# A routed expert stage on one core: where its visit map is made, how its shared map is spread, and in which order its merged tiles are stored

## What is computed

```python
mod = (_silu(c) @ wmod)                      # sa, ca, ga, sb, cb, gb per batch
h = _layernorm(x) * (1 + ca) + sa
x = x + ga * attention(h)                    # 16 heads, softmax over 256 tokens
h = _layernorm(x) * (1 + cb) + sb
logits = h @ router_w
e = argmax(logits);  weight = softmax(logits)[e]
hid = gelu(h @ w1[e] + b1[e])                # 128 -> 256
x = x + gb * weight * (hid @ w2[e] + b2[e])  # 256 -> 128
```

## Time and profile before

| | us |
|---|---|
| median of three runs | 622.87 |
| the profiled execution, its own time | 624.31 |
| its span, first to last instruction | 622.5 |
| VectorE busy | 564.3 (91%) |
| ScalarE busy | 542.3 (87%) |
| GpSimd busy | 483.0 (78%) |
| TensorE matmul busy | 471.1 (76%) |
| mean granted TensorE clock, share of full speed | 0.645 |

### The profile page before, as it was taken

The page is one execution under the profiler, slowest core; times in us unless marked ns, Lnnn a source line. Parts: engine busy times, 40 slices in busy tenths (PEclk is TensorE's granted clock), DMA queues, the critical chain, the costliest instruction groups (busy, mean ns, idle before and its releaser), DMA issues.

```text
span 622.5 us, 11883 instructions
## 1 busy us (share of the span) xinstructions
PE 471.1 (76%) x2535; PEld 265.6 (43%) x2537; DVE 564.3 (91%) x1432; ACT 542.3 (87%) x2310; POOL 483.0 (78%) x642
## 2 busy tenths in 40 slices
PE   5457877877887787788787887788776876799990
PEld 2113333433333343343343443343332465688980
DVE  5899999999999999999999999999999787878983
ACT  2599999999999999999999999999999745467760
POOL 4476777998899899999988999898887754567544
PEclk9555567566556756655556556655655589999996
DMA  6465454555555545554555456665553128857741
GB/s 190 106 185 149 135 137 129 151 148 150 148 155 147 157 143 150 144 153 141 140 141 145 135 148 178 181 169 155 152 168 127 51 97 222 274 176 203 230 124 34
DMA packets 77071, 94.41 MB, mean 152 GB/s; under 512 B 12806, under 2 KB 60710, under 8 KB 76998
## 3 DMA queue, kind: packets, MB, share of 16 engines
q1 hardware_dynamic: 68842, 75.69, 45.0%
q0 software_dynamic: 6144, 16.82, 7.2%
q10 hardware_dynamic: 2015, 1.15, 0.7%
HBM read 58.41 MB, written 35.20 MB: 150 GB/s over the span
## 4 chain that ended last, share of the span: by engine, by line
ACT 47%; POOL 18%; DVE 14%; issue 8%; PE 6%; DMA 4%; SPq 1%; DVEq 1%; ACTq 1%; POOLq 0%
ACT scores L887 46%; POOL table L804 3%; DVE neg_max L1339 3%; POOL xhat L753 2%; POOL rstd L736 2%; DVE y_biased_s L1910 2%; POOL rest L545 1%; POOL parts L548 1%; PE scores L1167 1%; DMA x_s<-table 1%; POOL out_dram L862 1%; PE scores L1176 1%; POOL h_scaled L776 1%; DMA table<-rows,place_i 1%; SPq L556 1%
## 5 line engine op out<-in xcount | busy, mean ns | idle before, releaser
L887 ACT ACTIVATE scores<-scores,neg_max 128x256 f32<-128x256 f32 x1024 | 467.5, 838 | 11.1 <-DVE neg_max L1339 11.0
L887 ACT ACTIVATION_READ_ACCUMULATOR scores<-scores,neg_max 128x1 f32 x1024 | 432.2, 599 | 0.0
L1339 DVE TENSOR_REDUCE neg_max<-scores 128x4 f32<-128x1024 f32 x256 | 309.2, 1211 | 7.1 <-PE scores L1019 6.5
L1019 PE MATMUL scores<-k_stack,q_stack 64*128 64x256 bf16 x1024 | 148.3, 388 | 79.0 <-ACT scores L887 68.5
L1019 PEld LDWEIGHTS scores<-k_stack,q_stack 64*128 64x128 bf16 x1024 | 33.9, 106 | 163.7 <-ACT scores L887 118.9
L804 POOL DMA_INDIRECT table<-rows,place_i x64 | 66.1, 1032 | 20.5 <-issue 17.1
L862 POOL DMA_INDIRECT out_dram<-out_room,x_s x51 | 49.8, 976 | 37.3 <-DVE out_room L1923 29.3
L1176 PE MATMUL scores<-w_s,hid 128*128 x308 | 50.5, 287 | 5.1 <-DVE y_biased_s L1910 3.2
L753 POOL TENSOR_SCALAR xhat<-rows,mv,rstd 128x128 f32<-128x128 f32 x60 | 47.5, 794 | 7.1 <-POOL rstd L736 7.1
L1047 PE MATMUL side_a<-w_gated,opt_t 128*128 128x128 f32 x128 | 49.8, 491 | 0.0
L745 POOL TENSOR_SCALAR xhat<-x_s,mv,rstd 128x128 f32<-128x128 f32 x62 | 49.0, 798 | 0.4 <-POOL rstd L736 0.4
(11 more groups left out here) (224 smaller groups left out, 878.7 us busy)
## 6 DMA issues: line engine op xcount, KB each, us to landing
x_s<-table SPq DMA_DIRECT2D x77, 192.5 KB, 3.0
q_stack<-parts_dram SPq DMA_DIRECT2D x192, 64.0 KB, 2.9
parts_dram<-parts SPq DMA_DIRECT2D x31, 384.0 KB
k_stack<-parts_dram SPq DMA_DIRECT2D x186, 64.0 KB, 2.3
mod_b<-mod_rows SPq DMA_DIRECT2D x32, 256.0 KB, 4.4
x_s<-in_x_dram SPq DMA_DIRECT2D x13, 256.0 KB, 5.0
table<-pad_tile SPq DMA_DIRECT2D x15, 192.5 KB
w1x_s<-in_w1x_dram SPq DMA_DIRECT2D x7, 258.0 KB, 4.6
```

The source lines that it names most:

```text
L887: last = act.activation(buf[:, k * L:k * L + L], buf[:, k * L:k * L + L], ACT.Exp, bias=neg_max[:, p, n:n + 1], accum_out=exp_sum[:, p, n: ...
L1019: last = pe.matmul(scores[:, c, at:at + L], q_stack[p][r, g + j, t * P:t * P + P], k_stack[p][r, g + j, :], start=True, stop=True)
L1339: dve.tensor_reduce(to, scores[:, (PAIRS * b.n + i) % RING, :].rearrange("p (e j m) -> p e j m", e=2, j=2), AX_X, ALU.max, negate=True).th ...
```

## The change

Three edits, and nothing of the arithmetic is altered.

1. **The map.** `map_counts()`, `map_rows()` and `map_columns()` leave tiles 6 to 8 and are run in `drain()`, behind `weigh_rows(last)` and the w1 fetch of visit 4, so ahead of DVE's share in visit 2. PE turns the map at the head of tile 7, DVE writes it out in tile 6.
2. **The shared map.** The same fourteen steps run one per tile in tiles 12 to 25. PE turns the result at the end of tile 28, DVE writes it out in tile 30.
3. **The stores.** Merged tile k waits for `min(k + 14, 2k + 2)` merges and stands in POOL's order directly behind the visit that brings that count; six merged tiles then stand between whole ones (visits 36 to 63), seven behind them (visits 64 to 76). Merged stores count on a semaphore of their own, for which SP waits last.

```diff
-MAP_TURNED = 9
-SHARED_AT = 15
-SHARED_TURNED = SHARED_AT + 9
+MAP_TURNED = 7
+SHARED_AT = 12
+SHARED_TURNED = SHARED_AT + 16
...
-def merged_by(slot):
+def merged_by(k):
-    return slot - WHOLE + E
+    return min(k + E, 2 * k + 2)
+def stores():
+    order, packed = [], 0
+    for q in range(NT):
+        f, v = VISITS[q]
+        if f is not None:
+            order.append((f, None))
+        while packed < PACKED and v is not None and merged_by(packed) == v + 1:
+            order.append((None, packed))
+            packed += 1
+    return order
...
-                sp.wait_ge(out_stored[s], 16 * len(range(s, T, SLOTS)))
+                sp.wait_ge(out_stored[s], 16 * len(range(s, WHOLE, SLOTS)))
+            sp.wait_ge(packed_stored, 16 * PACKED)
...
+            def store_packed(k):
+                pool.wait_ge(merged, merged_by(k))
+                pool.indirect_dma_start(out_rows, bass.IndirectOffsetOnAxis(ap=packed[:, k, D:OUT], axis=0),
+                                        packed[:, k, 0:D].bitcast(F32), None).then_inc(packed_stored, 16)
...
-            for n in range(FIRST, T):
-                store(n)
+            for n, k in STORES[FIRST:]:
+                if n is not None:
+                    store(n)
+                else:
+                    store_packed(k)
...
             def tile(j, s, turn):              # PE
+                if j == MAP_TURNED:
+                    turn_map()
                 if j == EARLY:
                     pe.wait_ge(map_ready, 1)
...
-                if j == MAP_TURNED:
-                    turn_map()
-                if j == SHARED_TURNED:
-                    turn_shared()
...
                     contract(j - AT_W2)
+                if j == SHARED_TURNED:
+                    turn_shared()
...
-                if j == MAP_TURNED:            # DVE
+                if j == MAP_TURNED - 1:
                     take_map()
...
-                    if n == FIRST:
-                        map_counts()
...
-                if j == SHARED_AT:
-                    shared_rest()
-                    shared_rest_f()
...
-                if n == PRIMED - 1:
-                    map_rows()
-                if n == PRIMED:
-                    map_columns()
+                steps_shared = (shared_rest, shared_rest_f, shared_places, shared_places_i, shared_split, shared_split_f, shared_spans,
+                                shared_before, shared_bounds, shared_low, shared_high, shared_in, shared_columns, shared_edges)
+                if 0 <= j - SHARED_AT < len(steps_shared):
+                    steps_shared[j - SHARED_AT]()
...
                 weigh_rows(last)               # DVE, drain
                 load_experts(PRIMED, EARLY - PRIMED)
                 fetch_w1(PRIMED)
+                map_counts()
+                map_rows()
+                map_columns()
```

More of the change, by code:

```diff
@@ L244, in shared_reload @@
     return min(SLOTS, SHARED - v) if v is not None and v % SLOTS == 0 else 0
-def merged_by(slot):
-    return slot - WHOLE + E
+def merged_by(k):
[10 more added lines that the diff above has]
+    return order
+STORES = stores()
+assert len(STORES) == T
 def early_slots(b):
@@ L508, in build_adaln_attention_moe @@
         merged = sem("merged")
+        packed_stored = sem("packed_stored")
         rows_loaded = [sem(f"rows_loaded{s}") for s in range(SLOTS)]
@@ L853, in store @@
             def store(n):
[L855 to L858, removed]
-                else:
[L860 to L863, removed]
-            over_batches(iteration, drain)
-            for n in range(FIRST, T):
-                store(n)
+                q = AT_VISIT[n]
+                pool.wait_ge(out_ready, q + 1)
+                pool.indirect_dma_start(out_rows, bass.IndirectOffsetOnAxis(ap=rows_in[q % SLOTS][:, ID:ROW].bitcast(I32), axis=0),
+                                        out_s[q % SLOTS][:, :], None).then_inc(out_stored[n % SLOTS], 16)
+            def store_packed(k):
+                pool.wait_ge(merged, merged_by(k))
+                pool.indirect_dma_start(out_rows, bass.IndirectOffsetOnAxis(ap=packed[:, k, D:OUT], axis=0),
+                                        packed[:, k, 0:D].bitcast(F32), None).then_inc(packed_stored, 16)
+            over_batches(iteration, drain)
+            for n, k in STORES[FIRST:]:
+                if n is not None:
+                    store(n)
+                else:
+                    store_packed(k)
         @block.scalar
```

## The result

The changed kernel took 615.98 us (median of six runs, 615.35 to 619.01), the kernel before beside it 622.61 (620.76 to 623.65): a ratio of 0.9902, 95% interval 0.9879 to 0.9926. The forecast was 615.7. The profiled execution of the changed kernel has a span of 613.5 and a time of its own of 615.35, the lowest of its six; that of before (624.31) lies above its median. The two profiles are thus 9.0 apart where the medians are 6.6 apart, and the sum has to be read from places inside them.

The account below looks back on a forecast made before the run. No engine is full in the visits; late rows bound visit 12, POOL's stores visit 48, POOL alone the end. Terms 0, -5.0, +0.5, -2.7 sum to -7.2: 624.31 becomes 617.1, median 615.7, range 612.0 to 620.3.

Parts of the forecast that it names:

- 0 for the map: Before visit 12: map about 2.9 us earlier, but the rows' scatter ends later, so no gain.
- -5.0: Shared map, visits 12 to 48: earlier single steps and later turn gain 5.0 us, bounds 3.5 to 6.7.
- +0.5: Six merged stores between whole ones push POOL's stores where it is backlogged: 0.5 us lost, bounds 0 and 2.5.
- -2.7: At the end, the last merged tile is stored right after the last merge: 2.7 us gained.
- the price of visits 7 to 11: TensorE before visit 12: five visits at 1.15 us each, 5.8, plus up to 0.9 waiting for a bias.
- the rival of the falling clock: TensorE stands longer before visit 12 and its clock falls, costing 2.1 us: 617.8 us; chance 8%.
- Visit 12 "well before 522": Sign of being wrong: visit 12 starting well before 522, where the forecast had its row wait ending near 522.8.
- POOL idled behind merged stores: Sign of being wrong: POOL idle behind merged stores while whole tiles are ready.
- load 38 waited for the shared map: Sign of being wrong: SP's load of visit 38 waiting for the shared map, despite a forecast cover of 1.6 us.
- The early scatter: Rival before visit 12: scatter lands before the map, visit 12 gains up to 2.9 more, 612.8 us; chance 8%.
- Only the end pays: Rival: w1 fetches or full DMA engines cancel the shared map's gain, leaving only the tail, 620.2 us; chance 13%.
- The slower rival: Merged stores waiting at the head of POOL's queue, 11.4 us in all, lose 9.0: 629.2 us; chance 5%.

Follow-up runs that it names:

- e2: Kernel before with the shared map's edit alone, old map place and old store order: 619.59 us, ratio 0.9949.
- e4: Changed kernel with all whole tiles stored first, then the merged ones at their new, lower merge counts: 615.87 us, ratio 0.9894.
- e3: Kernel before with the edit of the stores alone, map and shared map as before: 619.40 us, ratio 0.9946.
- e8: Changed kernel with the first six merged tiles stored later, five of them two whole tiles later and the last one: 617.54 us, ratio 0.9899.
- e10: Changed kernel with all whole tiles stored first and the shared map's steps begun in tile 8, turned in tile 24: 616.68 us, ratio 0.9880.
- e6: Changed kernel with the six pad blocks beside the last scatter moved, all fourteen written in visits 16 to 35: 620.42 us, ratio 0.9950.
- e9: Changed kernel with one more w1-sized copy on VectorE, into unused memory, in each of tiles 12 to 25: 619.23 us, ratio 0.9932.
- e1: Changed kernel with the map put back into tiles 6 to 8 and turned in tile 9: 617.10 us, ratio 0.9918.
- e5: Changed kernel with the shared map's steps back in tiles 15 to 22, up to two a tile, turn kept late: 619.44 us, ratio 0.9931.

## Why the prediction was right, and where not

**The sum.** The forecast was -7.2, of it 0 for the map, -5.0, +0.5, -2.7. Read from the places: -0.73 up to visit 12; store 32 -4.24 and visit 48 -4.11; from visit 48 to the end of the last merge +1.42 (40.88 to 42.30); from there to the last store -2.76 (3.13 to 0.37). That is -6.2, beside -6.6 between the medians. So the terms were off by -0.7, +0.9 (at visit 48), +0.9 and -0.1, 1.0 in all, and that 615.98 lies only 0.3 from the forecast median is in part luck. The stated bounds, 613.0 to 618.5, don't come out of the terms either: with 0 for the map their ends add up to -9.5 and -3.6, 613.4 to 619.3 on the median of 622.87.

**The map: the value was right, the reason half right.** The map did end earlier (written out at 511.85 instead of 517.55), and the stall fell from 3.18 to 0.70. The forecast said that the time comes back as a longer wait for visit 12's rows. That failed: the wait fell from 2.22 to 0.71. By the forecast's own figures TensorE was to be ready 8.3 us after the scatter's issue (520.9 - 512.55) and the rows 10.2 after it, 1.9 apart. Measured were 8.8 (518.55 - 509.77) and 9.5. So 0.7 of the missing cover is the quicker landing and what follows it, and 0.4 is TensorE. There the step at fault is the price of visits 7 to 11, 1.15 a visit. After the map's turn at 511.28 TensorE needed until 519.26 - 0.71 = 518.55, 7.3, where the forecast had 5.8 and up to 0.9 of waiting. In these stretches of after and of before:

```profile
510.00:514.00 4.00, 3.25 (x16) 2.53 (x16) 3.43 (x18) 1.29 (x5) 1.03 (x2) 0.50 1.03 296
```
```profile
510.00:514.00 4.00, 3.45 (x27) 3.05 (x27) 3.43 (x15) 2.40 (x10) 2.20 (x3) 1.00 0.55 187
```

the granted clock is 0.50, the lower level of 1.2 GHz, in after, and 1.00, 2.4 GHz, in before. So time went into slow visits in front of the wait, and the wait for the rows hid it from the end. It looks like the rival of the falling clock, earlier than it was put (ahead of visit 7, not of visit 12), but its reason, that TensorE now stands longer, is not shown. The same stretch of e2, whose map is late, and of e4, whose map is early:

```profile
510.00:514.00 4.00, 3.59 (x17) 3.59 (x18) 3.42 (x15) 2.05 (x9) 2.29 (x3) 0.50 0.48 170
```
```profile
510.00:514.00 4.00, 2.36 (x22) 1.88 (x20) 3.24 (x17) 1.25 (x5) 1.92 (x2) 1.00 0.57 202
```

The clock stands at either level with the map in either place. What lowers it there stays open.

**The signs of being wrong.** All three that the prediction named came, though the time was as forecast. Visit 12 "well before 522" came at 519.26; 2.8 of that came with the scatter and 0.73 with a quicker landing (5.65 for 6.39) and what follows it, so this sign, put in absolute time, said little. POOL idled behind merged stores, and load 38 waited for the shared map; both are taken up below.

**The shared map: the mechanism right, the gain smaller at the end.** No stall of 2.55 (e3 keeps it), the clock at 1.00 where before has 0.50 in 543 to 544; bias 8 to bias 22 took 539.66 - 520.64 = 19.02, forecast 19.5, before 23.47. Store 32 gained 4.24 beside a forecast of 4.9 and a term of 5.0. Alone the edit brings 4.0 to the last store in the profile and 2.9 between the medians (e2). TensorE and VectorE of after in that stretch (the same view):

```profile
538.00:541.00 3.00, 1.74 (x13) 1.43 (x12) 2.35 (x13) 0.92 (x5) 2.02 (x3) 1.00 1.00 299
541.00:544.00 3.00, 3.00 (x32) 2.79 (x31) 2.56 (x10) 2.19 (x8) 1.64 (x2) 1.00 0.80 244
```

The cover of load 38, 1.6 by the forecast, was not enough by a little: SP waited for the shared map's writing-out, which the list at the end of the prediction counts against it. The waits of SP in after (waited for: us in total, times, longest us):

```profile
SPq L549 <- DVE packed_now L1922: 1.2, 1, 1.2
```

It stayed without a consequence. TensorE shows no wait for rows at visit 38. The wait is 1.4 in e4, 1.1 in e8 and 0.4 in e2, which keep their gain, and absent in the changed kernel profiled again.

**The stores: the end right, the term in between too small.** The tail is as forecast, -2.76 for -2.7, and e3 shows it by itself. The term for the six stores in between was mis-sized: +0.5 was taken, +1.4 measured, inside the bounds of 0 to 2.5. Two things make it up. Four of the six merged stores did wait at the head of POOL's queue with whole tiles ready behind them (1.36, 1.18, 1.51 and 2.22, the whole stores following at 0.30; for the 1.51 the profile names no releaser). The step at fault is the wait that the text had called a fraction of a visit: it is one to two visits of 0.95. Its price stayed small, 0.4 to 0.9 by e8 and e4. And e2, e4 and e10, which store no merged tile there, still take 41.58, 41.83 and 41.31 from visit 48 to the last merge for 40.88 of before: 0.4 to 0.9 of an earlier visit 48 is lost on the way whatever the stores do, and belongs to the shared map's term. What takes it was not tried apart.

**The rivals.** The early scatter: the landing was 0.7 quicker, and e6, which made it some 3 quicker, gained nothing at visit 12. Only the end pays: e3 is that case made, 619.40. Its reason with the w1 fetches is there in small. Counted in all thirteen profiles from 515 on, 167 stores have such a copy starting within 0.13 us of their own start, and 119 of them take over 1.00 us; of the 628 others 37 do. The longest of after is 1.15, and with the two copies of e9 a store takes up to 1.27. After, a store and the copy that starts 0.04 behind its start:

```profile
537.64 1.15 POOL L876 DMA_INDIRECT out_dram<-out_room,x_s  x1 [0.30 <-issue]
```
```profile
537.68 0.28 DVE L1928 COPY w_ring<-w1x_s 128x258 f32 x1
```

Most stores take 0.95 to 0.96, also where a copy runs later in them, so this sets no pace. The Trainium skill ("SBUF — State Buffer", SBUF: two separate sides) has it that such a copy keeps GpSimd from writing descriptors; the traces agree for many of the copies at a store's start, at 0.19 us or less each in after, and not for those later in it. So the prediction, which read from two stores that the trace does not show it, said too much; that the fetches hold a store up for their whole length of 0.25 is not seen. The slower rival's waits are there, 6.3 us in four of the six where it had 11.4 in all, at a tenth of its price.

**What stays open.** Why the last scatter comes at about 510 in some profiles and at 512 to 513 in others. The clock in the hand-written end differs. Stretch of after, then of before:

```profile
495.00:498.00 3.00, 3.00 (x20) 2.00 (x19) 2.42 (x8) 1.30 (x5) 1.23 (x2) 0.96 0.18 66
```
```profile
495.00:498.00 3.00, 3.00 (x9) 1.47 (x8) 1.77 (x6) 1.91 (x4) 1.62 (x3) 0.50 0.18 66
```

It is 0.91 to 0.96 there in after, e1 and e3, which issue their last scatter at 509.8 to 510.0; 0.79, 0.70 and 0.63 in the changed kernel again, e9 and e8, at 510.5, 511.0 and 511.3; and 0.50 to 0.58 in the other seven, at 512.0 to 512.9. TensorE is busy all three us in all thirteen. Either place of the map and of the shared map stands on both sides. The four profiles with all whole tiles stored first (before, e2, e4, e10) stand on the late side only; but e4's runs are as fast as the changed kernel's (615.87 and 615.98), so I don't count it for the change, though it isn't ruled out. That e5 and e6 took 3.0 and 4.0 more than the changed kernel beside them, where their profiles show 0.9 to 1.7 and 1.0 to 1.8 behind visit 12, may mean that a kernel's runs lean to one side. What makes the clock rise early was not settled.

## What to carry to other kernels

A wait that is taken away pays only as far as the next thing that ends: list all of them at that place (here the rows behind a landing, a side computation, and the engine's own earlier work), each at the clock that may be granted. A side computation on the engine that sets the pace costs most of its length there (in e9 about two thirds or more); what can be won is the stall of its consumer, by placing that behind work which waits for the same engine anyway. Whether steps moved to where another engine sets the pace are free, e5 and e10 leave open. In a queue served in order, give late items weaker conditions first; standing them between ready ones brought nothing here, and cost some tenths in the profiles where they waited at the head.

## What of the hardware had not been expected

The clock's rise in the hand-written end came almost 3 us apart in the profiles of these kernels, and with it everything behind it moved, which is nearly half of the gain that was to be measured. And GpSimd's indirect stores, 0.95 to 0.96 us for the most part, are often longer, up to 1.15 in after, where a copy of VectorE starts together with them, and seldom otherwise. TensorE can run on at the lower level though it is hardly idle: in e6 it was busy 3.55 and 3.94 us of two stretches of 4, at 0.50 in both, with single-precision products of 128x128. All this rests on thirteen profiled executions of these kernels and is not a rule.
